# Sorted rows gathered out of x by an index list, experts started among the products, key chain spread over GpSimd, DVE and ACT

## What is computed

```python
# block 1: four experts, a token's expert from its id; gate, up and down weights are all ctx[e]
expert = minimum(clip(itok, 0, 12499) // 3125, 3)
g = silu(h @ ctx[e].T); u = h @ ctx[e].T
y = (g * u) @ ctx[e]                       # taken where expert == e
# block 2: fp8 product, one scale for all of h and one for the weight
h8, sh = quant_e4m3(h); w8, sw = quant_e4m3(w)
y = ((h8 @ w8.T) * (sh * sw)).astype(bfloat16)
# block 3: attention of 16 heads of 16 elements, 1024 queries against 1024 keys of ctx
q = (h @ Wq + bq) / 4; k, v = split(ctx @ Wkv + bkv)
q, k = fq_sym(q, axis=-1), fq_sym(k, axis=-1)      # to 127 steps per row and head
v = fq_sym(v, axis=keys)
p = fq_unsigned(softmax(q @ k.T), axis=-1)         # to 255 steps
y = (p @ v) @ Wp + bp
# block 4: ternary weight
y = h @ ternary(w).T + bias
```

## Time and profile before

| | |
|---|---|
| runs | 336.18, 336.62, 336.67 us; median 336.62 |
| the profiled execution | 335.34 us |
| its span, first to last instruction | 333.3 us |
| mean granted TensorE clock, share of full | 0.888 |
| TensorE busy, matmuls / weight loads | 230.9 us (69%) / 158.2 us (47%) |
| DVE busy | 268.4 us (81%) |
| ACT busy | 204.6 us (61%) |
| GpSimd busy | 171.8 us (52%) |

### The profile page before, as it was taken

How to read it: one execution, slowest core, us unless ns; L and a number is a source line. 1 busy time by engine, 2 the same in 40 slices (tenths; PEclk the granted TensorE clock), 3 DMA queues, 4 the chain that set the end, 5 groups by cost and what they waited for, 6 DMA issues and landing times.

```text
span 333.3 us, 6250 instructions
## 1 busy us (share of the span) xinstructions
PE 230.9 (69%) x2212; PEld 158.2 (47%) x2212; DVE 268.4 (81%) x401; ACT 204.6 (61%) x340; POOL 171.8 (52%) x291
## 2 busy tenths in 40 slices
PE   4890498595126867587877787787877878778670
PEld 4440266463014655055554455554555545557560
DVE  3553799978699896889999999999999999983850
ACT  1100125344524236989999999999999999993210
POOL 2360324476981700256555565555655556564634
PEclk9997559996555885959999999999999999999998
DMA  7924000029950000477988988797987998894011
GB/s 254 280 96 127 0 3 0 0 39 164 199 106 0 0 2 0 94 143 142 158 146 157 144 145 160 150 157 153 159 149 150 159 150 148 159 145 88 16 48 63
DMA packets 124303, 37.11 MB, mean 111 GB/s; under 512 B 118897, under 2 KB 123377, under 8 KB 124273
## 3 DMA queue, kind: packets, MB, share of 16 engines
q1 hardware_dynamic: 122176, 33.31, 55.1%
q0 software_dynamic: 768, 2.10, 1.8%
q10 hardware_dynamic: 1328, 1.32, 1.2%
HBM read 5.25 MB, written 2.10 MB: 22 GB/s over the span
## 4 chain that ended last, share of the span: by engine, by line
issue 31%; POOL 30%; DVE 16%; PE 10%; DMA 6%; ACT 5%; POOLq 0%; ACTq 0%; DVEq 0%
POOL gates L447 15%; POOL ebias L439 7%; DMA ksplit<-in_x 3%; PE ps L1081 3%; PE ps L1192 3%; POOL rstd L383 2%; POOL scratch L377 2%; DMA xs<-scratch 2%; DVE hs L880 2%; DVE stats L886 1%; POOL ksplit L409 1%; PE ps L1222 1%; POOL out L475 1%; ACT kv L588 1%; PE ps L1184 1%
## 5 line engine op out<-in xcount | busy, mean ns | idle before, releaser
L914 DVE TENSOR_REDUCE nmax<-ps 128x1 f32<-128x1024 f32 x128 | 153.2, 1223 | 10.1 <-PE ps L1208 7.1
L1208 PE MATMUL ps<-keysT,kv 128*128 128x512 bf16 x256 | 80.0, 396 | 40.3 <-ACT ctx L602 21.0
L602 ACT ACTIVATE ctx<-ps,ebias,qscale 128x1024 uint8<-128x1024 f32 x64 | 76.6, 1199 | 6.7 <-POOL ebias L439 5.3
L602 ACT ACTIVATE ctxT<-ps,ebias,qscale 128x1024 uint8<-128x1024 f32 x64 | 76.6, 1199 | 2.4 <-POOL ebias L439 1.2
L439 POOL TENSOR_SCALAR ebias<-nmax,qscale 128x1 f32<-128x1 f32 x128 | 33.8, 264 | 80.3 <-DVE nmax L914 73.9
L447 POOL CAST gates<-ksplit 128x1024 int16<-128x1024 uint8 x64 | 66.3, 1036 | 8.1 <-DMA ksplit<-ctxT 3.3
L1240 PEld LDWEIGHTS ps<-identb 128*128 128x128 bf16 x484 | 37.8, 99 | 29.6 <-issue 2.5
L1240 PE MATMUL ps<-identb 128*128 128x128 bf16 x484 | 47.8, 222 | 0.3 <-POOL gates L447 0.3
L1208 PEld LDWEIGHTS ps<-keysT,kv 128*128 128x128 bf16 x256 | 14.9, 98 | 55.8 <-ACT ctx L602 28.1
L506 ACT COPY hT<-ps 128x256 f32<-128x256 f32 x11 | 4.1, 372 | 45.9 <-PE ps L1073 45.9
L1247 PE MATMUL ps<-vals,gates 128*128 128x16 f16 x512 | 22.4, 170 | 0.0
(11 more groups left out here) (181 smaller groups left out, 360.7 us busy)
## 6 DMA issues: line engine op xcount, KB each, us to landing
ctx<-in_ctx SPq DMA_DIRECT2D x2, 512.0 KB, 4.8
ksplit<-in_x ACTq DMA_DIRECT2D x1, 1024.0 KB, 10.7
xs<-scratch SPq DMA_DIRECT2D x1, 1024.0 KB, 5.6
wkv_s<-in_L_xattn_Wkv SPq DMA_DIRECT2D x1, 512.0 KB, 8.3
ksplit<-ctx SPq DMA_TRANSPOSE x32, 3.7
ksplit<-ctxT SPq DMA_TRANSPOSE x32, 3.7
bkv_b<-in_L_xattn_bkv ACTq DMA_DIRECT2D x1, 256.0 KB, 11.1
wt_s<-in_L_ffn_weight SPq DMA_DIRECT2D x1, 256.0 KB, 9.6
```

The source lines that it names most:

```text
L602: a.activation(probs, s_in, ACT.Exp, bias=ebias[:, u % 4:u % 4 + 1], scale=qscale[:, t, u:u + 1], accum_out=lsum[:, t, u:u + 1]).then_inc( ...
L914: v.tensor_reduce(nmax[:, u % 4:u % 4 + 1], score_banks(k, u), AX.X, ALU.max, negate=True).then_inc(max_ready, 1)
L1208: last = m.matmul(ps[:, bank + b, :], qT[:, t, u // 2, :], keysT[:, u % 2, u // 2, 512 * b:512 * b + 512], start=True, stop=True)
```

## The change

**The sort.** The load of x, the scatter, the readback and the iota into `record` go. DVE splits `dest` into tile and lane by a shift and a mask and compares both with counting rows, `at_tile` (128x64) and `at_lane` (128x1024, in bf16); `ids` is `at_tile` times the token's number in two parts. TensorE makes 8 small products (L1111 of the new kernel), which leave the number of the token at each sorted place in PSUM, and DVE adds the two parts into `token_of`. GpSimd then gathers each tile of `xs` straight from x by `token_of` (L391), five tiles, then two and one with the first roots between.

**The start of the experts.** TensorE turns the second half of the context behind the index products. The registers of the tile experts are loaded behind the second product of keys and values (L1228). The first tile is turned before the eighth product. Sums and roots of the first norms are taken in groups (`ROOT_GROUPS`), tiles 0 to 2 normed by DVE, 3 to 7 by ACT; the last three tiles' sums stand in the steps 0 to 2 of the experts. The mains before the extra tiles are five instead of three.

**The gate.** ACT takes sigmoid and square out of PSUM, DVE multiplies the two in SBUF, one instruction instead of two.

**The key chain.** The product with the inverse scale moves to GpSimd (L438), the rounding on DVE to steps 5 and 6, ACT's casts to steps 8 and 10, the second roots (now in pairs of tiles) between the first difference (L444) and `klo` (L453). The clears are split, four blocks before the third roots and four behind them (L465). The rounding of the fp8 weight is in step 1, its turn in step 3 and 5; the ternary weight's steps move back.

The diff, cut to its core:

```diff
-FIRST_MAINS = 3
+FIRST_MAINS = 5
+EARLY_NORMS = 3
+ROOT_GROUPS = ((0, 1), (1, 3), (3, 5), (5, 7), (7, 8))
 QT_BY_DVE = (5, 7)
-KEY_PARTS = (4, 6)
-NORM_AT = 4
+KEY_PARTS = (8, 10)
+GATHERS_FIRST = 5
 PARTS = 3
 PAIRS = 4
+KEYS_FIRST = 4
 PT = 4
 UNPACK_LAG = 6
...
         def sums_step(t):
-            return FIRST_MAINS + E + 1 + t // 2 if t <= FIRST_MAINS else t + E + 1
+            return FIRST_MAINS + E + t // 2
...
-            sp.wait_ge(scattered, 16 * NT)
-            sp.dma_start(xs[:, :, :], sorted_v[:, :, 0:D]).then_inc(ld_sorted, 16)
-            sp.dma_start(token_of[:, :].unsqueeze(2), sorted_v[:, :, D:D + 1].bitcast(I32),
-                         allow_slow_non_contiguous=True).then_inc(ld_order, 16)
...
-            pool.wait_ge(dest_ready, 1)
-            pool.wait_ge(ld_x, 16)
-            for t in range(NT):
-                g.indirect_dma_start(scratch, bass.IndirectOffsetOnAxis(ap=dest[:, t:t + 1], axis=0),
-                                     record[:, t, :], None).then_inc(scattered, 16)
+            g.memset(ksplit[:, :, PARTS, :], 0.0).then_inc(consts, 1)
+
+            def gather(t):
+                g.indirect_dma_start(xs[:, t, :], None, x_rows,
+                                     bass.IndirectOffsetOnAxis(ap=token_of[:, t:t + 1], axis=0)).then_inc(gathered[t], 16)
...
+            def first_root(lo, hi):
+
+                pool.wait_ge(sums1_ready, hi)
+                if lo < EARLY_NORMS:
+                    inverse_root(lo, hi, rstd_ready)
+                    return
+                inverse_root(lo, hi)
+                for t in range(lo, hi):
+                    root = g.tensor_scalar(nmr[:, t:t + 1], mv[:, t, 0:1], rstd[:, t:t + 1], -1.0, ALU.mult, ALU.mult)
+                root.then_inc(rstd_ready, 1)
+
+            pool.wait_ge(token_ready, 1)
+            for t in range(GATHERS_FIRST):
+                gather(t)
+            first_root(*ROOT_GROUPS[0])
+            gather(GATHERS_FIRST)
+            gather(GATHERS_FIRST + 1)
+            first_root(*ROOT_GROUPS[1])
+            gather(GATHERS_FIRST + 2)
+            for lo, hi in ROOT_GROUPS[2:]:
+                first_root(lo, hi)
...
+            kk = kv[:, :, 0:D].rearrange("p r (h d) -> p r h d", d=HD)
+            pool.wait_ge(kinv_ready, 1)
+            for i in range(2):
+                part = slice(i * KT // 2, (i + 1) * KT // 2)
+                g.tensor_tensor(kq[:, part, :, :], kk[:, part, :, :],
+                                kinv[:, part, :].unsqueeze(3).broadcast_to([P, KT // 2, H, HD]), ALU.mult).then_inc(kdiv, 1)
...
+            for t in range(0, NT, 2):
+                pool.wait_ge(sums2_ready, t + 2)
+                inverse_root(t, t + 2)
+                for i in range(t, t + 2):
+                    g.tensor_scalar(nmr[:, i:i + 1], mv[:, i, 0:1], rstd[:, i:i + 1], -1.0,
+                                    ALU.mult, ALU.mult).then_inc(rstd2, 1)
             pool.wait_ge(kmid, 2)
             g.tensor_tensor(ksplit[:, :, 2, :], k3, ksplit[:, :, 1, :], ALU.subtract).then_inc(klo, 1)
-            for t in range(NT):
-                pool.wait_ge(sums2_ready, t + 1)
-                inverse_root(t, t + 1)
-                g.tensor_scalar(nmr[:, t:t + 1], mv[:, t, 0:1], rstd[:, t:t + 1], -1.0,
-                                ALU.mult, ALU.mult).then_inc(rstd2, 1)
...
+            def clear_keys(lo, hi):
+                for r in range(lo, hi):
+                    pool.wait_ge(keys_turned[r], 32)
+                    for a in range(2):
+                        if r + a:
+                            pool.wait_ge(keys_zeroed, 2 * r + a)
+                        other = slice(P // 2, P) if a == 0 else slice(0, P // 2)
+                        g.memset(keysT[other, a, :, r * P:(r + 1) * P].bitcast(F32), 0.0).then_inc(keys_zeroed, 1)
...
-
+            clear_keys(0, KEYS_FIRST)
+            pool.wait_ge(sums3_ready, 1)
+            inverse_root(0, NT // 2, rstd3)
+            pool.wait_ge(sums3_ready, 2)
+            inverse_root(NT // 2, NT, rstd3)
+            pool.wait_ge(rstd3, 2)
+            clear_keys(KEYS_FIRST, KT)
             pool.wait_ge(keys_zeroed, 2 * KT)
-            for k in range(2):
-                pool.wait_ge(sums3_ready, k + 1)
-                inverse_root(k * NT // 2, (k + 1) * NT // 2, rstd3)
...
+            def gates(j):
+
+                act.wait_ge(z_full, j + 1)
+                if j >= 2:
+                    act.wait_ge(gu_ready, j - 1)
+                a.activation(sig[:, j % 2, :], ps[:, j % 2, 0:D], ACT.Sigmoid).then_inc(gates_ready, 1)
+                a.activation(square[:, j % 2, :], ps[:, j % 2, 0:D], ACT.Square).then_inc(gates_ready, 1)
+
...
+            def first_norm(t):
+                act.wait_ge(rstd_ready, [k for k, (lo, hi) in enumerate(ROOT_GROUPS) if lo <= t < hi][0] + 1)
+                a.activation(hs[:, t, :], xs[:, t, :], ACT.Identity, bias=nmr[:, t:t + 1],
+                             scale=rstd[:, t:t + 1]).then_inc(h_late, 1)
...
-            v.tensor_copy(dest[:, :], dest_f[:, :]).then_inc(dest_ready, 1)
+            step(v.tensor_copy(dest[:, :], dest_f[:, :]))
+            v.tensor_scalar(dest_tile[:, :], dest[:, :], P.bit_length() - 1, None, ALU.arith_shift_right).then_inc(dve_done, 1)
+            n[0] += 1
+            step(v.tensor_scalar(dest_lane[:, :], dest[:, :], P - 1, None, ALU.bitwise_and))
+            dve.wait_ge(rowid_ready, 7)
+            step(v.tensor_tensor(at_tile[:, :, :], lane[:, 0:NT].unsqueeze(1).broadcast_to([P, NT, NT]),
+                                 dest_tile[:, :].unsqueeze(2).broadcast_to([P, NT, NT]), ALU.is_equal))
+            v.tensor_tensor(ids[:, :, :, :], at_tile[:, :, :].unsqueeze(2).broadcast_to([P, NT, 2, NT]),
+                            id_parts[:, :, :, :], ALU.mult).then_inc(ids_ready, 1)
+            v.tensor_tensor(at_lane[:, :, :], lane[:, :].unsqueeze(1).broadcast_to([P, NT, P]),
+                            dest_lane[:, :].unsqueeze(2).broadcast_to([P, NT, P]), ALU.is_equal).then_inc(ids_ready, 1)
...
+            dve.wait_ge(tokens_full, 1)
+            step(v.tensor_reduce(token_f[:, :], ps[:, 4, 0:2 * NT].rearrange("p (i t) -> p t i", i=2), AX.X, ALU.add))
+            v.tensor_copy(token_of[:, :], token_f[:, :]).then_inc(token_ready, 1)
...
 
+            weights(0)
+            dve.wait_ge(sched_ready, 1)
+            first_tiles = [dve.value_load(start_tile[0:1, e:e + 1], min_val=0, max_val=NT - 1) for e in range(E - 1)]
+            dve.wait_ge(ld_bkv, 16)
+            for r in range(3):
+                add_kv(r)
+            first_sums(0)
+            weights(1)
+            add_kv(3)
+            first_sums(1)
+            first_norm(0)
+            add_kv(4)
+            add_kv(5)
+            first_sums(2)
+            add_kv(6)
+            first_sums(3)
+            add_kv(7)
+            first_norm(1)
+            first_norm(2)
+            first_sums(4)
+            kk = kv[:, :, 0:D].rearrange("p r (h d) -> p r h d", d=HD)
...
             def background(s):
 
+                if s < 3:
+                    first_sums(s + 5)
+                if s == 1:
+                    weights(3)
+                if s == 5:
+                    weights(KT - 1)
                 if s == 0:
+                    dve.wait_ge(kv_ready, KT)
                     step(v.tensor_reduce(kmax[:, :, :], kk, AX.X, ALU.max, apply_absolute_value=True))
                     step(v.tensor_scalar(kscale[:, :, :], kmax[:, :, :], 1.0 / 127.0, 1e-8, ALU.mult, ALU.max))
-                    step(v.reciprocal(kinv[:, :, :], kscale[:, :, :]))
...
-                    step(v.tensor_tensor(kq[:, part, :, :], kk[:, part, :, :],
-                                         kinv[:, part, :].unsqueeze(3).broadcast_to([P, KT // 2, H, HD]), ALU.mult))
+                    v.reciprocal(kinv[:, :, :], kscale[:, :, :]).then_inc(kinv_ready, 1)
...
+                    part = slice((s - 5) * KT // 2, (s - 4) * KT // 2)
+                    dve.wait_ge(kdiv, s - 4)
                     k2 = kq[:, part, :, :].rearrange("p r h d -> p (r h d)")
                     v.tensor_scalar(k2, k2, ROUND, ROUND, ALU.add, ALU.subtract).then_inc(kround, 1)
-                if s in (3, 4):
...
             def gate(j):
 
-                z = ps[:, j % 2, 0:D]
-                dve.wait_ge(sig_ready, j + 1)
-                step(v.tensor_tensor(zz[:, j % 2, :], z, sig[:, j % 2, :], ALU.mult))
+                dve.wait_ge(gates_ready, 2 * j + 2)
                 if j >= 2:
                     dve.wait_ge(guT_full, j - 1)
-                v.tensor_tensor(gu[:, j % 2, :], z, zz[:, j % 2, :], ALU.mult).then_inc(gu_ready, 1)
+                v.tensor_tensor(gu[:, j % 2, :], square[:, j % 2, :], sig[:, j % 2, :], ALU.mult).then_inc(gu_ready, 1)
...
+            keys_values(0)
+            keys_values(1)
             pe.wait_ge(sched_ready, 1)
             tile_experts = [pe.value_load(tile_expert[0:1, t:t + 1], min_val=0, max_val=E - 1) for t in range(NT)]
```

(16 more changed lines are left out.)

219 lines of the change are left out of this document (115 added, 104 removed).

## The result

The changed kernel takes 338.89 us, median of 19 runs (336.55 to 341.34); the kernel before takes 336.07, median of 19. The ratio is 1.0084, with a 95% interval from 1.0064 to 1.0105: the change makes the kernel slower, by 2.8 us. I had forecast 333.1 and a range up to 338.5. The profiled execution took 339.28 us, with a span of 337.0.

The account below looks back on a forecast made before the run. Idle engines and a slow clock before the attention bound the kernel; -11.2 + 4.4 + 2.0 + 2.3 - 1.0 = -3.5 took the profiled 335.34 us to 331.8, or 333.1 for the median, range 327.5 to 338.5.

Parts of the forecast that it names:

- The start of the experts, -11.2: Up to the first gate multiply: gathers replace scatter and readback, gate at 30.1 instead of 41.34; bounds -14 to -8.
- The expert stage, +4.4: First gate to maximum over all tokens: 48.4 us instead of 44.0, from a longer GpSimd chain before second roots; bounds 0 to +8.
- the clock, +2.0: Expert stage: TensorE idles about 4 us for the key scale, so part of the expert work runs at 1.2 GHz.
- The held gate: Expert stage: DVE's gate, now with two SBUF inputs, can be held by GpSimd; one hold counted, 3.5 us.
- Behind the maximum, +2.3: Maximum to first head: rounding held +2.0, clears -0.6, third norms -2.0 and +0.5, query's scale held +3.6; bounds 0 and +4.
- the clock at the first heads, -1.0: Where attention begins: the clock was down 10.3 us there and its fall shifts; from 0 to -2, taken as -1.0.
- All that follows is the same code: From the first head maximum on, 204 us: the change does not work there.
- The port rival: Gates of steps 5 to 9: three long GpSimd operations fully in series with experts, 11.5 us, +8, so 341; chance 0.13.
- gates of 2 us and more: Expert stage: the sign named beforehand that would show the forecast wrong through the port.
- The clock rivals: Experts: clock stays up, 328.6, chance 0.20; or stays down until 50 us, +6.6 instead of +2.0, 337.7, chance 0.10.
- The keys are late: Before the first head: last clear or transpose ends last, if klo ends after about 88; 336 with klo at 91; chance 0.07.
- 0.19 for slower: Whole kernel: the chance given to the change measuring slower, against 0.76 for faster and 0.05 within 0.2%.

Follow-up runs that it names:

- experiment 10: Changed kernel with TensorE's tile-expert loads spread, one before the third product, the others two steps ahead of use: 337.66 us, ratio 1.0041.
- experiment 5: Changed kernel with DVE's copy of the fp8 weight's scale out of PSUM moved earlier, behind the fifth key and value product: 335.14 us, ratio 0.9965.
- experiment 1: Changed kernel with the gate as before, ACT taking the sigmoid alone and DVE multiplying twice out of PSUM: 336.64 us, ratio 1.0025.
- experiment 9: Changed kernel with all 16 clears of the turned keys before the third roots, as in the kernel before: 343.88 us, ratio 1.0255.
- experiment 11: Changed kernel with early keys, early weight-scale copy and bias additions in the attention, plus ternary rounding moved among the products: 327.95 us, ratio 0.9780.

## Why the prediction was wrong, step by step

The forecast for the profiled execution was 331.8; it took 339.28. At the maximum the kernel was 6.2 us behind the forecast of 78.5, and 1.6 of that was there at the first gate.

- **The start of the experts, -11.2.** Measured -9.6. Right in its mechanism and within its bounds: gathers cost what scatters cost, and TensorE's order sets the first gate (experiment 10 moved its loads, and the gate came 1.8 us earlier). The products start 1.9 us later than I had them, the loads' gap is 1.4 us smaller.
- **The expert stage, +4.4, and the clock, +2.0.** Measured 53.03 us against 43.97, +9.1, outside my bounds for the stage (0 to +8). This is where the prediction failed, and the step is the end of the first key difference: I had it at 68, with the roots from there, and it ended at 74.28. What lies behind it I had right, 10.5 us to the maximum; measured 10.45. The 6.3 us came in two parts. First, I had DVE's added work in steps 0 to 2 delay only the sums of the last tiles and so the extra tiles, "at about 46". I had TensorE idle for about 4 us there (measured 3.85), but put that down to the clock alone and didn't follow what waits on DVE's work from the other side: the fp8 weight's scale, moved behind the key scale, keeps a PSUM bank that the first turned gate needs. The extra tiles were there at 49.9, 3.9 us late, and 3.0 of that was the bank (experiment 5: 46.86). Second, from there to the second rounding it took 9.2 us, not 7.7, and from GpSimd's product to the difference 7.4, not 6: the held 128x2 scale stood in front of gate 7, and ACT's first cast behind the copy of that gate, at 64.70, though the product was over at 62.83. My working also has 4 us from the multiplies to the rounding with no row for them, and its terms add up to 67.4, not 68. The +2.0 for the clock isn't in the trace: its mean over the stage is 0.82, before 0.81.
- **The held gate.** I had put one hold in the sum, 3.5 us. Two gates and the 128x2 scale were held, by 2.85, 0.8 and 3.25 us, so 6.9; the kernel before had 2.3 of that kind in its stage (the row at 60.26). My reason against more, that operations with one SBUF input "ran through before", was a misreading: that row has one. Taking the gates' holds away (experiment 1) gave 2.0 us of the whole, of which 0.9 or nothing is at the maximum; where the rest comes from isn't shown.
- **Behind the maximum, +2.3, and the clock at the first heads, -1.0.** Together +1.3, measured +1.9. The places are right: the fp8 rounding held, the norms at 2.55 instead of 3.39, the query's scale held twice. The -1.0 isn't in the trace, the clock is 0.50 at the first heads as before.
- **"All that follows is the same code"** stood for 0, and the profiled execution was 2.4 us longer there. 1.4 of it is one more fall of the clock, which some versions' traces show and others don't. Whether the change has a part in it is open. The changed kernel's runs fall in two groups, eight from 336.5 to 338 and ten from 338.8 to 339.8, with one at 341.3.
- **The rivals.** The port rival came nearest, 341, but as a number by luck. Its mechanism is in the trace, and its sign, gates of 2 us and more, came once (3.27). The rule it goes by (the Trainium skill, GPSIMD Engine Reference, Key points) agrees with the rows for the gates: held at 3.27 us with two SBUF inputs, free at 0.42 out of PSUM. But the held time was 6.9 us, not the rival's 11.5, just short of the 7.0 from which it decides, and 2.85 of it lay beside the difference, for which ACT and the roots waited anyway. The loss needed the bank as well, and that I had in no rival. The clock rivals are out: over the experts the clock was neither better nor worse than before (0.82 and 0.81), and the kernel was slower all the same. "The keys are late" was out in its form: the last difference was over at 86.8, and DVE never waited for the transposes; but they were 15 us later than before, and experiment 9 shows what that would have cost without the split.

My 0.19 for slower was too low: each of my rivals was one mishap, and here several small delays added up in one chain on GpSimd, with no rival for their sum.

## What to carry to other kernels

When work is moved up in front of other work, ask for each small operation that now stands behind it what it frees: a register, a semaphore, and above all a bank or buffer; a 0.13 us copy held back TensorE and ACT here, and GpSimd behind them. An operation that several engines wait for (here the key difference) can't be mended from one side: taking the gate off it gave 0.9 us at the maximum, no more than two traces of the same code differ by, taking the cast off it too gave nothing more, and moving the operation gave 2.1. Look for the wait that all versions share: here the maximum came 9.7 to 10.4 us behind the start of the second roots in every one. A held operation is a loss only if nothing else would have waited in its place. And measure the parts alone: the gather was worth 1.1%, all of it hidden in a change that came out slower.

## What the runs showed of the hardware

- A long GpSimd tensor_tensor on SBUF can hold even the smallest DVE operation until it ends: 128x2 with one SBUF input took 3.42 and 3.68 us instead of 0.17 (2.49 in the kernel before), a 128x256 multiply of two SBUF inputs 3.27 and 3.41 instead of 0.42. Statistics of a tile in SBUF, which lay under the same operation, ran through (0.40 at 70.77 in the changed kernel), and so did multiplies with one input in PSUM (0.42) and, beside the bias addition, a reciprocal of 128x64 (0.55) between two held operations of that size (1.67 instead of 0.20).
- The hold passes to the next operation in line if that is of a kind that can be held: in experiment 11 the gate took 3.41 us in place of the 128x2 operation, and nothing was won.
- An indirect gather of 128 rows of 1 KB takes GpSimd 0.95 us and 0.30 between (0.97 and 0.30 for the scatter of these rows with their number).
